# A two-layer graph kernel: the degree sums divided between VectorE and GpSimd by halves of the sums

## The reference

```
A = 0.5 * adj ; A[i,i] += 0.5                      # layer 0
x1 = layernorm(x + relu(((A / A.sum(axis=1)) @ x) @ W.T + b))
t  = logmap0(x1)                                   # layer 1
par = adj   * sigmoid(t@w_par[:128] [:,None] + t@w_par[128:] [None,:] + b_par)
chi = adj.T * sigmoid(t@w_chi[:128] [:,None] + t@w_chi[128:] [None,:] + b_chi)
out = layernorm(x1 + proj(expmap0(chi @ t + par @ t)))
```

## Time and profile before

| | |
|---|---|
| median of 3 runs | 2198.63 us (2198.61 to 2199.72) |
| the profiled execution | 2200.13 us, its span 2198.3 us |
| busy: PE, VectorE, GpSimd, ACT | 2006.2, 1929.8, 1340.4, 1318.0 us |
| moved by DMA | 820.37 MB, 373 GB/s in the mean |
| degree sums on VectorE | 594.1 us (240 of 2048 columns) and 27.0 us (16 of 1024) |
| fold on GpSimd | 18.8 us (8) |

### The profile page before, as it was taken

One profiled execution on the slowest core, in us unless ns is written; L12 is line 12 of the kernel. 1 busy time (PEld: TensorE's weight loads), 2 busy tenths in 40 slices (PEclk: granted clock), 3 DMA queues, 4 the chain that ended last, 5 costly groups with the idle time before them and its releaser, 6 DMA issues. The chain is left out here.

```text
span 2198.3 us, 18369 instructions
## 1 busy us (share of the span) xinstructions
PE 2006.2 (91%) x5072; PEld 898.4 (41%) x5072; DVE 1929.8 (88%) x1864; ACT 1318.0 (60%) x1508; POOL 1340.4 (61%) x639
## 2 busy tenths in 40 slices
PE   7999999999999998999999978898888888889886
PEld 3444444444444444444444433343333333334333
DVE  5757787988989989898999989999998998989896
ACT  0001324454464454454453588988989988989996
POOL 0000304534455554644544677999998998999996
PEclk9999999999999999999999988999999999999998
DMA  9978988989989989988989998999999999999993
GB/s 338 362 273 291 400 288 349 406 343 384 388 329 409 414 331 363 392 337 337 416 345 348 422 408 329 421 420 421 422 410 421 421 419 394 421 421 398 398 393 143
DMA packets 128453, 820.37 MB, mean 373 GB/s; under 512 B 14880, under 2 KB 27488, under 8 KB 31328
## 3 DMA queue, kind: packets, MB, share of 16 engines
q1 hardware_dynamic: 113392, 799.06, 90.7%
q10 hardware_dynamic: 14960, 20.13, 2.7%
HBM read 814.88 MB, written 4.26 MB: 373 GB/s over the span
## 5 line engine op out<-in xcount | busy, mean ns | idle before, releaser
L548 POOL TENSOR_TENSOR chi<-chi,ring 128x1024 f32<-128x1024 f32 x326 | 834.4, 2573 | 628.5 <-ACT chi L756 572.4
L1244 PE MATMUL ps<-keys,xtA 128*128 128x512 f32 x2048 | 981.3, 611 | 140.1 <-DVE keys L1045 110.5
L1171 PE MATMUL ps<-ring,xA 128*128 128x512 f32 x2048 | 918.4, 598 | 33.8 <-DMA xA<-in_x_g 15.2
L773 ACT ACTIVATE ps<-scores,prcr 128x1024 f32<-128x1024 f32 x492 | 544.2, 1106 | 394.2 <-DVE keys L1045 377.5
L1244 PEld LDWEIGHTS ps<-keys,xtA 128*128 128x128 f32 x2048 | 377.6, 193 | 683.8 <-issue 653.0
L935 DVE TENSOR_TENSOR dsum<-dsum,ring 128x2048 f32<-128x2048 f32 x240 | 594.1, 2475 | 30.4 <-DMA ring<-in_g_blk 24.4
L1171 PEld LDWEIGHTS ps<-ring,xA 128*128 128x128 f32 x2048 | 387.5, 192 | 519.1 <-issue 493.9
L1045 DVE TENSOR_TENSOR keys<-ps,chi 128x1024 f32<-128x1024 f32 x426 | 521.6, 1225 | 85.6 <-issue 31.3
L756 ACT ACTIVATE chi<-scores,prcr 128x1024 f32<-128x1024 f32 x426 | 483.8, 1136 | 16.3 <-DMA scores<-plcl_d 8.5
L1036 DVE TENSOR_TENSOR ps<-ps,ring 128x1024 f32<-128x1024 f32 x348 | 425.5, 1223 | 44.4 <-ACT ps L773 39.0
L548 POOL TENSOR_TENSOR chi<-chi,xA 128x1024 f32<-128x1024 f32 x79 | 185.7, 2366 | 18.4 <-ACT chi L756 18.4
(11 more groups left out here) (122 smaller groups left out, 820.9 us busy)
## 6 DMA issues: line engine op xcount, KB each, us to landing
ring<-in_g_blk SPq DMA_DIRECT2D x443, 1024.0 KB, 8.6
ring<-in_a_cols SPq DMA_DIRECT2D x190, 1024.0 KB, 10.0
xA<-in_a_cols SPq DMA_DIRECT2D x51, 1024.0 KB, 11.9
xA<-in_g_blk SPq DMA_DIRECT2D x44, 1024.0 KB, 10.0
scores<-in_a_cols SPq DMA_DIRECT2D x15, 1024.0 KB, 11.7
scores<-in_g_blk SPq DMA_DIRECT2D x15, 1024.0 KB, 10.7
scores<-plcl_d ACTq DMA_DIRECT2D x22, 512.0 KB, 10.4
xA<-in_x_g ACTq DMA_DIRECT2D x64, 64.0 KB, 11.8
```

Of the source, the lines that this page charges most:

```text
L548: pool.tensor_tensor(out=chi(n), in0=chi(n), in1=half(t, n), op=ALU.mult).then_inc(m2_ready, 1)
L773: act.activation(dst, scores[:, row, 0, :], ACT.Sigmoid, bias=prcr[:, 2 * jt:2 * jt + 1]).then_inc(p_ready, 1)
L1171: ins = pe.matmul(Y[:, h * BANK:(h + 1) * BANK], xA[:, tile * D:(tile + 1) * D], t[:, tt * BP + h * BANK:tt * BP + (h + 1) * BANK], start= ...
L1244: ins = pe.matmul(outp[:, h * BANK:(h + 1) * BANK], xtA[:, jt * D:(jt + 1) * D], keys(n)[:, h * BANK:(h + 1) * BANK], start=begins, stop=i ...
```

## The change

GpSimd now makes the degree sums of pairs 0, 8, 16 and 24 of each panel, and VectorE those of the other 28. GpSimd adds only into the upper half of `dsum`, VectorE only into the lower half. So a pair is no longer added by one instruction of 2048 columns but by two of 1024, one per tile, the second of which waits for the first (they write the same columns): 27 such pairs and one single instruction (pair 1) per panel on VectorE, 3 such pairs and one single instruction (pair 0) on GpSimd. On GpSimd the sum stands behind the fold and ahead of the second product of the same pair. SP waits for the engine that made the pair's sum. `sums_done` counts for each pair how many sums each engine has then made. The fold waits for both engines.

```diff
+POOL_SUMS = (0, 8, 16, 24)
+def sums_done(g):
+    r, q = divmod(g, PPP)
+    theirs = r * len(POOL_SUMS) + sum(k <= q for k in POOL_SUMS)
+    return g + 1 - theirs, theirs
...
                     sp.wait_ge(l0_used, j + 1)
-                    sp.wait_ge(deg_added, j + 1)
+                    if j % PPP in POOL_SUMS:
+                        sp.wait_ge(deg_pool, sums_done(j)[1])
+                    else:
+                        sp.wait_ge(deg_added, sums_done(j)[0])
...
             def fold(r):
-                pool.wait_ge(deg_added, (r + 1) * PPP)
+                pool.wait_ge(deg_added, sums_done((r + 1) * PPP - 1)[0])
+                pool.wait_ge(deg_pool, sums_done((r + 1) * PPP - 1)[1])
...
+            def degree_sums(g):
+                r, q = divmod(g, PPP)
+                t, here, count = loaded("pair", g)
+                pool.wait_ge(here, count)
+                if q == 0:
+                    pool.wait_ge(folded, r)
+                    pool.tensor_tensor(out=half(dsum, 1), in0=half(t, 0), in1=half(t, 1), op=ALU.add).then_inc(deg_pool, 1)
+                    return
+                pool.wait_ge(deg_pool, sums_done(g)[1] - 1)
+                pool.tensor_tensor(out=half(dsum, 1), in0=half(dsum, 1), in1=half(t, 0), op=ALU.add).then_inc(deg_pool_half, 1)
+                pool.wait_ge(deg_pool_half, sums_done(g)[1] - r - 1)
+                pool.tensor_tensor(out=half(dsum, 1), in0=half(dsum, 1), in1=half(t, 1), op=ALU.add).then_inc(deg_pool, 1)
...
+                if q in POOL_SUMS:
+                    degree_sums(g)
                 if g in UNIT_AT:
                     second_product(UNIT_AT[g])
...
-                if q < 2:
-                    if q == 0:
-                        dve.wait_ge(folded, r)
-                    else:
-                        dve.wait_ge(deg_ready, r)
-                    dve.tensor_tensor(out=half(dsum, 1 - q), in0=half(t, 0), in1=half(t, 1), op=ALU.add) \
-                        .then_inc(deg_added, 1)
+                lower = half(dsum, 0)
+                if q == 1:
+                    dve.wait_ge(deg_ready, r)
+                    dve.tensor_tensor(out=lower, in0=half(t, 0), in1=half(t, 1), op=ALU.add).then_inc(deg_added, 1)
                     return
-                dve.wait_ge(deg_added, g)
-                dve.tensor_tensor(out=dsum[:, :], in0=dsum[:, :], in1=t, op=ALU.add).then_inc(deg_added, 1)
+                done = sums_done(g)[0]
+                dve.wait_ge(deg_added, done - 1)
+                dve.tensor_tensor(out=lower, in0=lower, in1=half(t, 0), op=ALU.add).then_inc(deg_half, 1)
+                dve.wait_ge(deg_half, done - r - 1)
+                dve.tensor_tensor(out=lower, in0=lower, in1=half(t, 1), op=ALU.add).then_inc(deg_added, 1)
...
-                degree_sums(g)
+                if q not in POOL_SUMS:
+                    degree_sums(g)
```

More of the change, by code:

```diff
@@ L397, in adj_resnorm_kernel @@
         deg_added = sem("deg_added")
+        deg_half = sem("deg_half")
+        deg_pool = sem("deg_pool")
+        deg_pool_half = sem("deg_pool_half")
         folded = sem("folded")
```

## The result

| | before | after |
|---|---|---|
| median, each of 4 runs | 2198.62 us (2198.38 to 2199.72) | 2249.53 us (2246.48 to 2251.82) |
| the profiled execution, its span | 2200.13, 2198.3 us | 2251.82, 2250.0 us |

The changed kernel is slower by 50.9 us, ratio 1.0225 [1.0212, 1.0238]. The direction was as predicted, the size was not: 2249.5 us against a forecast of 2214 and a range up to 2234. More than two thirds of the loss (35 us) is missing from the forecast's sum.

The account below looks back on a forecast made before the run. PE bounds the panels at 5.15 us per pair with a unit, plus its waits. Splitting 11.8, less 2.8, plus port 7.3 gives 16.3 us on 2200.13: 2216.4, less 1.5 for the median, stated as 2214; range 2195 to 2234.

Parts of the forecast that it names:

- What bounds the kernel: Panels: PE back to back, 5.15 us per pair with a unit; above it PE's waits on ring loads and `taken`.
- Splitting: VectorE's sums ahead of the stops in panels 3 to 7: two halves cost 0.20 us more per pair, 11.8 us.
- the opening: Boundary between VectorE's halves: GpSimd's product gets the port, key 1.46 us later, once per panel, 7.3 us.
- one insertion per panel: GpSimd getting in between two halves, from none to three times per panel (0 to 22 us); one was taken.
- Sums no longer made: VectorE's dropped sums: freed time mostly ends in waits; key at pair 8 0.56 us earlier, 2.8 us of gain.
- the forecast wait for ACT: Pair 8: the 2.20 us VectorE saves come back as a longer wait of `first_product` for ACT, about 2.4 us.
- Rival A: VectorE gains: the raw 2.35 us per panel arrives on the path, waits shrink by 12 us, 2187; chance 0.15.
- GpSimd's additions: Seven additions per panel, 16.5 us, have room on GpSimd, at pair 8 in its idle time; taken as 0.
- The port section: VectorE's two-source SBUF instructions and GpSimd's exclude each other; each boundary between halves is an opening; 7.3 us taken.
- the gap where VectorE catches up: Stretch without units in panels 3, 6 and 7, holding pair 16, where VectorE was said to catch up.
- rival C: Much slower, the port decides: three insertions per panel (22 us), split 11.8, less 2.8: 31 us, 2230; chance 0.2.
- late addition at pair 8: GpSimd's additions at pair 8 run late if the load lands late; 4.7 us each, 23 us at most.

Follow-up runs that it names:

- The square: Four kernels, whole sums or halves, each without and with GpSimd's six additions; against the kernel before: whole +2.3 and +35.5 us, halves +17.6 and +50.9 us.
- halves alone: Kernel before, with VectorE making all 30 wide sums of a panel in two chained instructions and GpSimd none: 2222.48 us, +23.2, ratio 1.0104.
- fills: Kernel before plus, for each of GpSimd's seven extra additions per panel into an unread tile, three fills of that tile instead: 2213.69 us, +14.4, ratio 1.0067.
- the additions of pairs 0 and 24: Kernel before, VectorE's sums unchanged, GpSimd also making only the additions of pairs 0 and 24 into an unread tile: 2213.97 us, +13.8, ratio 1.0065.

## Why the prediction was wrong

**What bounds the kernel.** Half right. That the loss would sit in panels 3 to 7, and that PE's idle time there is not won back, held (49.9 of 51.7 us in the profiled executions). That it would come through late loads did not: waits for loads rose by 1 to 3 us, those for keys and for `taken` and `xtA` by 30.

**Splitting, 0.20 us a pair, 11.8 us**, and **the opening, 7.3 us**: together 19.1. The square gives 15.3 for both; "halves alone", with three more split pairs per panel, 23.2, of which the chaining is 12.5. The mechanism is right, and so is the size within the noise, in part by luck: the forecast took one insertion per panel, and "halves alone" has second halves of 3.2 us at two or three pairs ahead of the stop (9 and 11, in panels 4 and 5 also 14; in panel 3, 8 and 11), so each cost less than the 1.46 us put on it. An undisturbed sum takes 2.40 us to the next instruction, as in the forecast. The opening looks otherwise than I said: the halves start 1.25 us apart, and the waiting stands inside the second half (3.25 us in pair 11); the product takes 2.70 us there in place of the 4.4 of a product behind a whole sum.

**Sums no longer made, a gain of 2.8 us.** Without GpSimd's six additions nothing is gained (+2.3 us, net of the addition of pair 0 and a longer fold). At pair 8 the freed time became the forecast wait for ACT, 2.43 us. Rival A, which had the relief arrive on the path and the kernel gain, falls: the kernel is 50.9 us slower.

**GpSimd's additions: "I take 0."** This is the step that failed: six of them per panel cost 33 us. The forecast asked whether there is room on GpSimd, and there was: 93 of 179 us busy. It did not ask who else uses the port while the additions run. The port section counted only the sums' new openings to the products, though the earlier trace rows show what a GpSimd instruction does to one of eight columns: 2.30 us. (The forecast calls it an addition; L548 is the second product, but an addition is as long.) It also put each addition beside the work of its own pair. In fact GpSimd ran ahead: the additions of pair 8 met the sum of pair 7, and those of pair 16 met, in panels 3, 6 and 7, the small instructions of pair 13, in what the forecast called the gap where VectorE catches up, with a stop of PE of 4.7 us in each. Each addition takes 2.36 us of a port which a sum and a product already use for 4.64 of 5.15 us, a number that the forecast had worked out for rival C. With the additions priced at the measured 33 us, the forecast would have been about 2247.

**Rival C** named the right resource, the port, and stood at 2230 since it too put the price on openings. Its late addition at pair 8 did not come: in panel 5 GpSimd waited 0.40 us for the load. The addition ran early and met the sum of pair 7.

The Trainium skill (SBUF — State Buffer, Who interferes with whom) says of the shared port pair that it is locked for a whole instruction, and that a VectorE instruction with two SBUF inputs collides with a GpSimd instruction that reads SBUF, not with one that only writes. The runs agree: fills left the sums at 396.6 us where additions made 421.7 of them. The same section of the Trainium skill lists `tensor_scalar` among those which can take the shared pair; the 0.86 and 0.97 us beside fills fit that, though no run here shows by which port they were held.

**Open:** what part of the fills' 14.4 us is queue, what the relief is worth without the longer fold, and how the 13.8 us of the additions of pairs 0 and 24 divide between the sum of pair 0 and the rest.

## What to carry to other kernels

An idle engine is not an idle resource: before work is moved from VectorE to GpSimd, add up the time both spend on instructions that need the shared port, and price each moved addition at up to its own length wherever the other engine's critical chain stands, also ahead of the pair to which it belongs. Here 4.64 of every 5.15 us were taken. The six additions that three of every 32 sums became cost 33 us, 1.1 us for each addition of 2.36, and VectorE's relief did not pay for them. And an instruction with a competitor for its port was better long than split here, since each seam let the other engine in.

## What the runs showed of the hardware

- The wait for the port stood inside the duration of the waiting instruction and not in the idle time ahead of it: 3.25 to 3.41 us for a half of 1.22, 2.30 for eight columns of 0.17, 4.48 for a whole sum of 2.28. No view of waits lists it; only the durations show it.
- With both engines ready all the time, the port went back and forth instruction by instruction (851.10 to 857.81 in the kernel after), so a sum in two halves met two GpSimd instructions where a whole one meets one.
- A TENSOR_SCALAR of VectorE, which has one source, in float32 on eight columns, was held by GpSimd's fills (0.86 and 0.97 us in place of 0.17), although a fill reads nothing; sums of two sources were not (2.28 us over three fills).
- Two halves of 1024 columns start 1.25 us apart when the second waits for the first, and 1.13 us when it does not: the wait cost 12.5 us over the kernel, uncertain by 5.
